# Swapping the stationary and the moving operand of an expert's gate and up products, and scatters two in flight

## What is computed

```python
probs = softmax(x @ gate_w.T)                     # 16 experts
vals, idx = top_k(probs, 4);  w = vals / sum(vals)
act = silu(x @ gate_e) * (x @ up_e)               # gate, up: 512 -> 384
out = sum over the 4 chosen e of w_e * (act @ down_e)      # down: 384 -> 512
out = out + the same with the weights of one shared expert, for all tokens
result = x + tanh(g_ffn) * out
```

## Time and profile before

| | |
|---|---|
| median of 3 runs | 735.83 us (734.85 to 740.84) |
| the profiled execution's own time | 733.4 us |
| span of its instructions | 731.6 us |
| mean granted clock of TensorE | 0.94 |

### The profile page before, as it was taken

The page is one execution under the profiler, slowest core; times in us unless marked ns, Lnnn a source line. Parts: engine busy times, 40 slices in busy tenths (PEclk is TensorE's granted clock), DMA queues, the critical chain, the costliest instruction groups (busy, mean ns, idle before and its releaser), DMA issues.

```text
span 731.6 us, 17952 instructions
## 1 busy us (share of the span) xinstructions
PE 631.8 (86%) x4586; PEld 387.6 (53%) x4587; DVE 525.2 (72%) x1299; ACT 316.9 (43%) x542; POOL 319.1 (44%) x504
## 2 busy tenths in 40 slices
PE   4112769999999699999999999999999999899992
PEld 3012445666656366556555565555555555565660
DVE  5999778877598586768887867688678888767210
ACT  2333573222234345455444454554444554445441
POOL 1464620000113454546456455554656455465532
PEclk9655769999999899999999999999999999999997
DMA  7661135110216679485866866767585776655432
GB/s 226 214 185 50 68 102 138 59 58 2 73 31 174 148 170 185 90 205 99 187 146 140 205 126 153 164 126 185 118 172 120 174 190 113 167 96 98 83 48 39
DMA packets 48524, 93.73 MB, mean 128 GB/s; under 512 B 7677, under 2 KB 15339, under 8 KB 48498
## 3 DMA queue, kind: packets, MB, share of 16 engines
q0 software_dynamic: 16128, 38.35, 29.6%
q1 hardware_dynamic: 32370, 55.07, 25.2%
HBM read 65.16 MB, written 28.24 MB: 128 GB/s over the span
## 4 chain that ended last, share of the span: by engine, by line
DMA 48%; PE 27%; DVE 10%; POOL 5%; issue 4%; ACT 2%; POOLq 2%; SPq 1%; DVEq 0%; ACTq 0%
DMA out<-mix_room,idx_s 46%; PE gu_ps L1113 15%; PE bank L1140 6%; DVE stats L671 2%; PE bank L1166 2%; POOL idx_s L480 2%; POOL pool_tick L458 2%; PE bank L1127 1%; DMA room_b<-token_rows,idx_g 1%; POOL mix_room L410 1%; POOLq L462 1%; DVE wgu L872 1%; PE bank L1152 1%; DMA out<-X 1%; ACT xT L532 1%
## 5 line engine op out<-in xcount | busy, mean ns | idle before, releaser
L1113 PE MATMUL gu_ps<-wgu,mix_room 128*128 x1728 | 305.4, 327 | 1.7 <-DVE tick L895 1.7
L1113 PEld LDWEIGHTS gu_ps<-wgu,mix_room 128*128 128x128 f16 x1728 | 166.4, 98 | 113.1 <-issue 8.0
L1140 PE MATMUL bank<-wdn,aT 128*128 (+1 forms) x792 | 186.1, 380 | 1.4 <-ACT aT L570 1.0
L570 ACT ACTIVATE aT<-bank 128x768 f16<-128x768 f16 x88 | 71.3, 810 | 144.1 <-PE bank L1127 137.1
L483 POOL DMA_INDIRECT out<-mix_room,idx_s x72 | 120.2, 1669 | 19.3 <-issue 19.1
L1140 PEld LDWEIGHTS bank<-wdn,aT 128*128 128x128 f16 x792 | 77.7, 98 | 86.6 <-issue 4.2
L939 DVE SCALAR_TENSOR_TENSOR act<-gu_ps,wslot,sg x72 | 44.5, 618 | 93.9 <-ACT sg L556 82.8
L467 POOL COPY idx_g<-room_b 128x1 int32 x72 | 56.1, 780 | 120.0 <-issue 100.1
L480 POOL COPY idx_s<-room_b 128x1 int32 x72 | 16.6, 230 | 192.1 <-DMA out<-mix_room,idx_s 164.3
L563 ACT ACTIVATE acth<-act 128x384 f16<-128x384 f32 x88 | 46.0, 523 | 120.6 <-DVE act L939 111.0
L470 POOL DMA_INDIRECT room_b<-token_rows,idx_g x72 | 78.1, 1084 | 11.2 <-issue 1.7
(11 more groups left out here) (156 smaller groups left out, 665.1 us busy)
## 6 DMA issues: line engine op xcount, KB each, us to landing
dn_sc<-dn_scale_halves SPq DMA_DIRECT2D x34, 384.0 KB
dn_raw<-in_L_ffn_down_packed SPq DMA_DIRECT2D x48, 256.0 KB
gu_sc<-gu_scale_halves SPq DMA_DIRECT2D x34, 192.0 KB
X<-in_x SPq DMA_DIRECT2D x4, 1024.0 KB, 11.6
token_rows<-room_a SPq DMA_DIRECT2D x16, 256.0 KB, 2.1
out<-X SPq DMA_DIRECT2D x4, 1024.0 KB, 4.5
gu_raw<-in_L_ffn_gate_up_packed SPq DMA_DIRECT2D x16, 192.0 KB
gu_raw<-in_L_ffn_gate_up_packed SPq DMA_DIRECT2D x16, 191.9 KB
```

The costliest lines, as they stand in the source:

```text
L570: nc.scalar.activation(aT[:, b].rearrange("p a c t -> p (a c t)"), at_ps, ACT.Copy).then_inc(aT_done, 1)
L1113: mm = nc.tensor.matmul(ps[b][:, 0:I], x(xp * HC + c), wgu[:, w, wp, c, col:col + I], start=(c == 0 and xp == 0 and wp == 0), stop=(c == H ...
L1140: mm = nc.tensor.matmul(y_ps[b][:, :], aT[:, b, ap, t, :], wdn[:, w, wp, t, :], start=(n == 0), stop=(n == 3 * IC - 1))
```

## The change

Gate and up are computed transposed. A 128x128 block of `wgu` is loaded as weights and the 128 columns of tokens stream against it; the gate's three blocks of 128 outputs come first (half 0), then the up's (half 1), 36 matmuls each. `transpose_act` and `copy_aT` go, since `act` comes out with its features on the partitions; the two halves are written straight into `aT`. The token is then not on the partitions, so the routing weight moves to the evacuation of y, where ACT picks it by the slot's expert (`take_weight`, with a `value_load` of its own). `down` waits for the halves itself. The one semaphore `added` becomes two, for even and odd slots; a scatter waits for the one two slots back, and for those before its expert's first slot, by a number from a third row of `slot_i`. The diff, without declarations, the constant `odd_s`, the renamed scales of the shared expert and the deleted calls in PE's shared loop:

```diff
--- before
+++ after
@@ -195,12 +194,13 @@
         TILES_ROOM = 2 * KMAX
         first_tiles_i = sb("first_tiles_i", [P, E], I32)
         pairs_i = sb("pairs_i", [P, 1], I32)
-        slot_f = sb("slot_f", [P, 2, SLOTS], F32)
-        slot_i = sb("slot_i", [P, 2, SLOTS], I32)
+        slot_f = sb("slot_f", [P, 3, SLOTS], F32)
+        slot_i = sb("slot_i", [P, 3, SLOTS], I32)
+        odd_s = sb("odd_s", [P, SLOTS], F32)
         iota_s = sb("iota_s", [P, SLOTS], F32)
         idx_g = sb("idx_g", [P, 2], I32)
         idx_s = sb("idx_s", [P, 2], I32)
-        wslot = sb("wslot", [P, 2, E], F32)
+        wslot = sb("wslot", [P, 2], F32)
         xTs = xn.rearrange("p b h -> p (b h)").bitcast(F16).rearrange("p (b n) -> p b n", b=2)
         y_sb = xmix
...
@@ -208,7 +208,6 @@
         gu_ps = psum("gu_ps", [P, 4, 512], F32)
         bank = [gu_ps[:, i, :] for i in range(4)] + [psum(f"bank{i}", [P, 512], F32)[:, :] for i in range(4, 8)]
         g_ps, u_ps = bank[0:2], bank[2:4]
-        at_ps = bank[4][:, 0:IC * P].bitcast(F16)
         y_ps = bank[5:7]
         sj_ps = bank[0:4]
...
@@ -281,7 +279,7 @@
         xTs_done = sem("xTs_done")
         wslot_done = sem("wslot_done")
         yev_done = sem("yev_done")
-        added = sem("added")
+        added = [sem("added0"), sem("added1")]
         idx_g_ready = sem("idx_g_ready")
         idx_s_ready = sem("idx_s_ready")
...
@@ -470,18 +468,23 @@
                 nc.gpsimd.indirect_dma_start(xg[:, b, :], None, rows_dram[:, :],
                                              bass.IndirectOffsetOnAxis(idx_g[:, b:b + 1], 0)).then_inc(xg_ld[b], 16)
 
-            def add(s, b):
+            def add(s, b, all_before=False):
 
                 col = pool.value_load(slot_i[0:1, 1, bass.ds(s, 1)], min_val=0, max_val=E * KMAX)
                 pool.wait_ge(yev_done, s + 1)
+                if not isinstance(s, int) or s >= 2:
+                    pool.wait_ge(added[b], 8 * (s - b))
                 if not isinstance(s, int) or s >= 1:
-                    pool.wait_ge(added, 16 * s)
+                    others = pool.value_load(slot_i[0:1, 2, bass.ds(s, 1)], min_val=16, max_val=8 * SLOTS)
+                    pool.wait_ge(added[1 - b], others)
+                if all_before:
+                    pool.wait_ge(added[1 - b], 8 * (s + b))
                 pool.wait_ge(st_out, 16 * (B + 1))
                 nc.gpsimd.tensor_copy(idx_s[:, b:b + 1], tok[:, bass.ds(col, 1)]).then_inc(idx_s_ready, 1)
                 pool.wait_ge(idx_s_ready, s + 1)
                 hold_wait()
                 nc.gpsimd.indirect_dma_start(out[:, :], bass.IndirectOffsetOnAxis(idx_s[:, b:b + 1], 0), y_sb[:, b, :],
-                                             None, compute_op=ALU.add).then_inc(added, 16)
+                                             None, compute_op=ALU.add).then_inc(added[b], 16)
             for s in range(4):
                 gather(s, s % 2)
             for b in range(2):
@@ -492,8 +495,9 @@
                     gather(2 * j + b + 2, b)
                     add(2 * j + b - 2, b)
             for k in range(-4, 0):
-                add(2 * inner + 4 + k, k % 2)
-            pool.wait_ge(added, 32 * inner + 64)
+                add(2 * inner + 4 + k, k % 2, all_before=k == -1)
+            for b in range(2):
+                pool.wait_ge(added[b], 16 * inner + 32)
 
         @block.scalar
...
@@ -559,32 +559,29 @@
             def high_halves(s, b):
                 a.wait_ge(act_done, s + 1)
                 if not isinstance(s, int) or s >= 2:
-                    a.wait_ge(at_done, s - 1)
-                nc.scalar.activation(acth[:, b, 0, :], act[:, b, :], ACT.Copy).then_inc(ah_done, 1)
-
-            def copy_aT(s, b):
-
-                a.wait_ge(at_done, s + 1)
-                if not isinstance(s, int) or s >= 2:
                     a.wait_ge(y_done, s - 1)
-                nc.scalar.activation(aT[:, b].rearrange("p a c t -> p (a c t)"), at_ps, ACT.Copy).then_inc(aT_done, 1)
+                nc.scalar.activation(aT[:, b, 0].rearrange("p c t -> p (c t)"), act[:, b, :], ACT.Copy).then_inc(ah_done, 1)
 
             def take_rows(r, b):
 
-                a.wait_ge(xg_ld[b], 8 * (r - b) + 16)
-                if not isinstance(r, int) or r >= 2:
-                    a.wait_ge(act_done, NT + r - 1)
-                nc.scalar.activation(wslot[:, b, :], xg[:, b, H:ROW], ACT.Copy).then_inc(wslot_done, 1)
                 a.wait_ge(tx_done, r + 1)
                 if not isinstance(r, int) or r >= 2:
-                    a.wait_ge(gu_done, NT + r - 1)
+                    a.wait_ge(u_done, NT + r - 1)
                 nc.scalar.activation(xTs[:, b, :], xT_ps, ACT.Copy).then_inc(xTs_done, 1)
+
+            def take_weight(r, b):
+
+                e = a.value_load(slot_i[0:1, 0, bass.ds(r, 1)], min_val=0, max_val=E - 1)
+                if not isinstance(r, int) or r >= 2:
+                    a.wait_ge(yev_done, r - 1)
+                nc.scalar.activation(wslot[:, b:b + 1], xg[:, b, bass.ds(H + e, 1)], ACT.Copy).then_inc(wslot_done, 1)
 
             def take_y(r, b):
                 a.wait_ge(y_done, NT + r + 1)
+                a.wait_ge(wslot_done, r + 1)
                 if not isinstance(r, int) or r >= 2:
-                    a.wait_ge(added, 16 * (r - 1))
-                nc.scalar.activation(y_sb[:, b, :], y_ps[b][:, :], ACT.Copy, scale=1.0 / W_SCALE).then_inc(yev_done, 1)
+                    a.wait_ge(added[b], 8 * (r - b))
+                nc.scalar.activation(y_sb[:, b, :], y_ps[b][:, :], ACT.Copy, scale=wslot[:, b:b + 1]).then_inc(yev_done, 1)
 
 
...
@@ -594,22 +591,22 @@
             a.wait_ge(lg_ps_ready, NT)
             nc.scalar.activation(lgh[:, :, :], lg_ps[:, :].rearrange("p (t k e) -> p t k e", k=2, e=E)[:, :, 1, :],
                                  ACT.Copy).then_inc(lgh_ready, 1)
-            copy_aT(0, 0)
             a.wait_ge(lsub_ready, 1)
             nc.scalar.activation(r_exp[:, :, :], lg[:, :, :], ACT.Exp).then_inc(exp_ready, 1)
             for i in range(2, NT):
-                copy_aT(i - 1, (i - 1) % 2)
+                gate(i, i % 2)
                 if i == NT - 1:
                     take_rows(0, 0)
-                activate(i, i % 2)
+                high_halves(i, i % 2)
             a.wait_ge(route_ready, 1)
             inner = a.value_load(pairs_i[0:1, 0:1], min_val=E // 2 - 2, max_val=SLOTS // 2 - 2)
 
             def slot(r, b, rows=True):
-                copy_aT(r + (NT - 1), 1 - b)
+                take_weight(r, b)
+                gate(NT + r, b)
                 if rows:
                     take_rows(r + 1, 1 - b)
-                activate(NT + r, b)
+                high_halves(NT + r, b)
                 if not isinstance(r, int) or r >= 1:
                     take_y(r - 1, 1 - b)
...
@@ -798,6 +794,10 @@
                     step(nc.vector.tensor_copy(slot_i[:, 0, :], slot_f[:, 0, :]), wait=False)
                 else:
                     step(nc.vector.tensor_reduce(slot_f[:, 1, :], slot_nt, AX, ALU.add))
+                    step(nc.vector.tensor_tensor(slot_f[:, 2, :], slot_f[:, 1, :], odd_s[:, :], ALU.add))
+                    step(nc.vector.tensor_scalar(slot_i[:, 2, :], slot_f[:, 2, :], 8.0, None, ALU.mult))
+                    step(nc.vector.tensor_scalar(slot_i[:, 2, :], slot_i[:, 2, :], 0xFFF0, None, ALU.bitwise_and))
+                    step(nc.vector.tensor_scalar(slot_i[:, 2, :], slot_i[:, 2, :], 16, None, ALU.max))
                     step(nc.vector.scalar_tensor_tensor(slot_f[:, 1, :], slot_f[:, 0, :], float(KMAX), slot_f[:, 1, :],
                                                         ALU.mult, ALU.subtract))
...
@@ -931,21 +931,26 @@
             dequant(0, 0, None, PARTS - 1)
             end_dequant(0)
 
-            def activations(s, b, weight):
+            def activations(s, b):
 
                 if not isinstance(s, int) or s >= 2:
-                    v.wait_ge(at_done, s - 1)
+                    v.wait_ge(ah_done, s - 1)
+                    v.wait_ge(al_done, s - 1)
                 v.wait_ge(sg_done, s + 1)
-                nc.vector.scalar_tensor_tensor(act[:, b, :], gu_ps[:, 2 + b, 0:I], weight, sg[:, b, :], ALU.mult,
-                                               ALU.mult).then_inc(act_done, 1)
+                v.wait_ge(u_done, s + 1)
+                nc.vector.scalar_tensor_tensor(act[:, b, :], gu_ps[:, 2 + b, 0:I], 1.0 / (X_SCALE * W_SCALE), sg[:, b, :],
+                                               ALU.mult, ALU.mult).then_inc(act_done, 1)
 
             def low_halves(s, b):
                 v.wait_ge(ah_done, s + 1)
-                nc.vector.tensor_tensor(acth[:, b, 1, :], act[:, b, :], acth[:, b, 0, :], ALU.subtract).then_inc(al_done, 1)
+                if not isinstance(s, int) or s >= 2:
+                    v.wait_ge(y_done, s - 1)
+                nc.vector.tensor_tensor(aT[:, b, 1].rearrange("p c t -> p (c t)"), act[:, b, :],
```

(63 more changed lines are left out.)

5 lines of the change are left out of this document (removed).

## The result

The changed kernel takes 916.91 us in the median of 4 runs (914.98 to 922.68), the kernel before 735.34 us beside it. The ratio is 1.247, 95% interval [1.239, 1.255]. The forecast was 922 us, slower.

What follows compares the result with a forecast made beforehand. PE's sequencer was to become the bound at 9.6 us a slot: 212.4 + 691 + 16.9 less 1 gives 919 us of span, 922 forecast; range 870 to 1000, slower with chance 0.88.

Steps and rivals of the forecast that it cites:

- What bounds the kernel: Kernel before: PE first at 6.63 us a slot, serial scatters close second, PE's sequencer third at 5.67 us a slot.
- The array's work: Routed slots on PE: at 55.7 ns a load and matmul pair, a slot goes from 6.63 to 6.41 us.
- The sequencer's work: PE's sequencer, routed slots: 48 register addresses make gate/up 6.2 us in place of 2.15, so 9.6 us a slot.
- What else changes: Outside PE's matmuls: paired scatters worth nothing at 9.6 us a slot; added register loads and later gather lie in slack.
- Shared slots: Fourteen slots with static addresses: 6.18 us each less 0.22, 3.1 us in all, 2 kept; first routed gate at 212.4.
- the sum: Whole span: first routed gate 212.4, 72 x 9.6 = 691, end 16.9, less 1, giving 919 us.
- The end: After down of slot 70: last slot's act, its down and last scatter stay at 16.9 us.
- the 1123 us: Rival, chance 0.07: PE's clock falls as the array idles in short gaps; slot 12.4 us, kernel 1123 us.
- Addresses are free: Rival, chance 0.10: register addresses of weight loads cost no sequencer time; array bounds the slot at 6.41, kernel 700 us.
- late gathers: Term in the 700 us rival: gathers that come later show on PE at 0.1 us a slot.

Runs made afterwards that it cites:

- fixed_weights: Changed kernel with the routed slots' gate/up blocks read from fixed addresses in xT, so without their register operations: 753.03 us, ratio 1.024 to the kernel before.
- tokens_loaded_128: Kernel before, own orientation, each 384-column gate/up matmul cut into three of 128 columns, so 48 register addresses a slot on the moving operand: 931.43 us, 1.265.
- addresses_32: Changed kernel with the third output block of gate and up read from fixed addresses, 32 register addresses a slot in place of 48: 797.08 us, 1.083.
- branch_on_parity: Changed kernel with PE's routed gate/up and down written for each weight-buffer half, a branch on the expert's parity picking one, addresses static: 763.31 us, 1.036.
- serial_with_load: Changed kernel with every scatter waiting for all before it, but the second register load on POOL kept: 918.21 us, 1.248.
- serial_scatters: Changed kernel with every scatter waiting for all before it, and the second register load on POOL gone: 941.4 us, 1.279.

## Why the prediction was right

**What bounds the kernel.** The sequencer as third resource, with under 1 us of slack, was the reading that decided. Nothing else in the page would have shown it, since PE, DVE and DMA all had room or gained some.

**The array's work.** 55.7 ns a pair was right, in rows of 72 too, and 6.41 us a slot for the array: 4.02 for the 72 pairs, 1.94 for down, 0.45 for the transposes. The page "TensorE: Matmul & The Clock Gate" of the Trainium skill, Back-to-back issue gap, gives about 81 ns for a sustained stream of pairs at 128 columns. No run here shows that; the measured 55.8 ns decides. The changed kernel's own 78 ns looks like that figure, and fixed_weights shows that it isn't: it is the sequencer's pace.

**The sequencer's work.** 48 addresses a slot, 3456 in all, and 9.6 us a slot came out as forecast. The 48 of one slot start from 635.4 to 641.7 us, 6.3 us with the transposes' step among them (forecast 6.2). tokens_loaded_128 confirms that the price hangs on the count, addresses_32 that it is near 0.11 us for each, fixed_weights and branch_on_parity that without it some 160 us are gone.

**What else changes.** That pairs of scatters are worth nothing here was right (serial_with_load). That the extra register loads on POOL cost nothing was right for POOL, but their place in time matters to PE, which I had not thought of (serial_scatters).

**Shared slots.** The profiled execution has its first routed gate at 214.48, not 212.4. Its first layer ran 5 us later from the start, though. In fixed_weights, where gate and up of the shared expert begin at 78.1 us as in the kernel before (78.3), the first routed gate comes at 210.47 against 214.36. So 3.9 us were gained, not 2. That the profiled span, 921.0 us, is so near the 919 of the sum is in part luck, then: the spans of the other executions, without the late first layer, are 913.3 to 916.0.

**The end.** From the last register load to the span's end it is 921.0 - 892.8 = 28.2 us; one slot and a wait are in it. By the sum's own terms: 214.5 + 72 x 9.60 = 905.7, and 15.3 remain, 15.9 forecast (16.9 less 1).

**The rivals.** The clock stayed at its upper level (1.00 granted) from 219 to 908 us, all of the routed slots but the first, with the array fed for two thirds of the time, so the 1123 us did not come. "Addresses are free" was false in the changed kernel. Its price was wrong too: 700 forecast, 753 in fixed_weights. The mis-sized term is the 0.1 us a slot for "late gathers". Taken over the 72 slots, the surplus over the plain steps is 24 us from up to down, 6 from down to gate and 19 from gate to transposes (gathers), 49 us or 0.68 a slot. Another 0.15 a slot lies inside the rows of up, gate and down: the clock fell six times in these slots, for 24 us in all. I had taken for granted that a sequencer with less work than the array stays hidden. It stays hidden only if its longest single delay fits into what is queued, and the change cuts that from 1.7 to under 1 us.

## What to carry to other kernels

Before making matmuls smaller or turning their operands round, count the different register-dependent addresses in each stretch and set their price (in these kernels about 0.12 us each, on either operand) against the array's time; the busy shares don't show the sequencer, its lines in the trace do. If the register has few values, write the code for each and branch: this took 154 of 182 us back. With short matmuls the queue holds less time, so each register read or branch needs a place of its own with queued work ahead of it; two in one place show up as "issue" at the next matmul.

## What the runs showed of the hardware that was not expected

- A register load on PE takes 0.30 us, and mostly 0.6 to 0.95 us when it starts 2 to 3 us after a scatter's instruction on POOL. This holds in all twelve traces: from 236 us on, 194 of the 238 loads that start in this time last over 450 ns, and of the 1427 others 6, all within 1 us after a gather's instruction. Shifting POOL by one register load moved the whole kernel from 918 to 941 us. What makes the load slow beyond this coincidence in time was not tried.
- The longest lead of PE's sequencer is a number of instructions and not a time: 17 matmuls with their weight loads, which was 0.93 us with 128 columns and 3.06 us with 384 and 512. What sets that number stays open.
- Executions differ by 5 us in the first layer. The same two fp32 matmuls of 512 columns at 17 us take 2.05 us in the profiled execution of the changed kernel and 1.10 in that of serial_scatters, with a granted clock of 1.00 recorded in both. This puts everything behind it 5 us later:

```profile
17.08 2.05 PE L1080 MATMUL gu_ps<-room_b,wj_all 128*128 128x512 f32 x2
...
83.29 0.95 PE L1119 MATMUL gu_ps<-xT,wgu 128*128 128x128 f16 x7
```
```profile
16.95 1.10 PE L1077 MATMUL gu_ps<-room_b,wj_all 128*128 128x512 f32 x2
...
78.06 2.23 PE L1116 MATMUL gu_ps<-xT,wgu 128*128 128x128 f16 x19
```

  The recorded clock thus doesn't show the pace of the first 28 us, and in the changed kernel's profile not up to 83 us either: the eight transposes ahead of the shared gate take 1.04 us in both traces, at 82.45 with 1.00 recorded and at 77.22 with 0.50. So the execution with the higher mean clock on record (0.988 against 0.950 to 0.957) is the slower one. The late first layer explains why the profiled execution of the changed kernel (922.68) is above the median, and why two profiles that differ by 5 us should first be laid over one another at 80 us.
